# A selective-scan layer on one core: bank readers, copies and stages moved, and TensorE's add of the state's product ahead of the jobs in every step

## The reference

```python
t = windows of x                               # (1024, 64, 128)
tn = layernorm(t) * ln_g + ln_b
xi, z = split(tn @ W_in + b_in)                # 256 channels each
xc = silu(causal_conv4(xi) + conv_b)
dr, Bm, Cm = split(xc @ W_x)                   # 8, 16, 16
delta = softplus(dr @ dt_w + dt_b)
h = exp(delta * A) * h + (delta * xc) * Bm     # 16 states per channel, over 64 tokens
y = sum over states of h * Cm, + xc * D
out = (y * silu(z)) @ W_out + b_out + x
```

## Time and profile before

| | us |
|---|---|
| median of 3 runs | 9951.25 (9944.27 to 9953.19) |
| the profiled execution's own time | 9964.25 |
| its span | 9962.4 |
| busy in the span: PE | 8796.7 (88%) |
| DVE | 8381.0 (84%) |
| POOL | 8037.3 (81%) |
| ACT | 7716.3 (77%) |
| mean granted TensorE clock | 0.976 |

### The profile page before, as it was taken

How to read it: one execution, slowest core, us unless ns; L and a number is a source line. 1 busy time by engine, 2 the same in 40 slices (tenths; PEclk the granted TensorE clock), 3 DMA queues, 4 the chain that set the end, 5 groups by cost and what they waited for, 6 DMA issues and landing times. The chain is left out here.

```text
span 9962.4 us, 180628 instructions
## 1 busy us (share of the span) xinstructions
PE 8796.7 (88%) x54525; PEld 6817.5 (68%) x54525; DVE 8381.0 (84%) x8272; ACT 7716.3 (77%) x13798; POOL 8037.3 (81%) x3609
## 2 busy tenths in 40 slices
PE   7888888888888888888888888888889999999899
PEld 4666666666666666666666666666678888888788
DVE  5888888888888888888888888888978888888766
ACT  5888888888888888888888888888845555555577
POOL 5888888888888888888888888888868888888600
PEclk8999999999999999999999999999999999999999
DMA  3333333333333333333333333333310110101165
GB/s 88 106 105 111 104 103 108 107 106 103 106 109 106 103 107 109 106 103 106 107 107 106 106 105 106 105 103 108 104 41 30 34 34 30 34 30 34 56 189 181
DMA packets 648651, 933.96 MB, mean 94 GB/s; under 512 B 79960, under 2 KB 277600, under 8 KB 643552
## 3 DMA queue, kind: packets, MB, share of 16 engines
q1 hardware_dynamic: 647904, 924.64, 29.5%
HBM read 778.38 MB, written 146.04 MB: 93 GB/s over the span
## 5 line engine op out<-in xcount | busy, mean ns | idle before, releaser
L1022 POOL TENSOR_TENSOR prod<-state,c_all 128x1024 f32<-128x1024 f32 x1280 | 3027.4, 2368 | 820.2 <-DVE state L895 792.1
L603 PEld LDWEIGHTS y_acc<-ident,prod 128*128 128x128 f32 x16384 | 1924.0, 144 | 844.7 <-issue 822.8
L895 DVE TENSOR_TENSOR_SCAN state<-decay_d,drive_d 128x1024 f32<-128x1024 f32 x1024 | 2338.0, 2283 | 187.7 <-ACT decay_d L731 156.8
L1011 POOL TENSOR_TENSOR drive_d<-du,b_all 128x1024 f32<-128x1024 f32 x1024 | 2423.7, 2367 | 0.0
L895 DVE TENSOR_TENSOR_SCAN state<-decay_r,drive_r 128x1024 f32<-128x1024 f32 x1024 | 2330.2, 2276 | 3.5 <-issue 1.4
L603 PE MATMUL y_acc<-ident,prod 128*128 128x128 f32 x16384 | 2195.5, 278 | 4.0 <-DVE prod L906 1.9
L1303 DVE SCALAR_TENSOR_TENSOR sum_d<-bank_d,filt,sum_d 128x512 f32<-128x512 f32 x2470 | 1679.5, 744 | 271.3 <-PE bank_d L1211 248.7
L744 ACT ACTIVATE ub<-ut,bt 128x256 f32<-128x256 f32 x4096 | 1737.1, 497 | 41.9 <-issue 28.7
L1350 POOL TENSOR_TENSOR sum_p<-sum_p,scaled 128x1024 f32<-128x1024 f32 x650 | 1554.6, 2392 | 261.0 <-ACT scaled L1261 229.0
L1261 ACT ACTIVATE scaled<-bank_p,filt 128x512 f32<-128x512 f32 x1560 | 945.5, 689 | 737.4 <-PE bank_p L1211 621.4
L590 PE MATMUL drive_r<-ident,ub 128*128 128x128 f32 x8192 | 1127.3, 282 | 344.9 <-DVE state L895 283.4
(11 more groups left out here) (155 smaller groups left out, 14649.4 us busy)
## 6 DMA issues: line engine op xcount, KB each, us to landing
c_all<-bc_rows SPq DMA_DIRECT2D x1280, 256.0 KB, 3.3
b_all<-bc_rows SPq DMA_DIRECT2D x1024, 256.0 KB, 3.6
ys<-row_spectra SPq DMA_DIRECT2D x130, 256.0 KB, 2.8
column_sums<-tt SPq DMA_DIRECT2D x130, 256.0 KB, 2.1
x_in<-in_x_dram SPq DMA_DIRECT2D x64, 512.0 KB, 4.8
x_res<-in_x_dram SPq DMA_DIRECT2D x64, 512.0 KB, 4.4
x_rows<-x SPq DMA_DIRECT2D x64, 512.0 KB, 4.3
row_spectra<-z SPq DMA_DIRECT2D x64, 512.0 KB, 4.8
```

What stands on the lines that cost most here:

```text
L603: mm = pe.matmul(y_acc[:, g, hf * P:(hf + 1) * P], prod[n % NP][:, hf, g * P:(g + 1) * P], wt["ident"][:], start=(n % NS == 0 and hf == 0 ...
L895: dve.tensor_tensor_scan(state[n % NT][:].rearrange("p h t -> p (h t)"), decay[:].rearrange("p h w t -> p (h w t)"), drive[:].rearrange("p ...
L1011: pool.tensor_tensor(drive_d[place_of(DSTEPS, n, ND)][:], du[:, :, q * HT:(q + 1) * HT], b_all[slot][:].unsqueeze(1).to_broadcast([P, 2, HT]),
L1022: pool.tensor_tensor(prod[n % NP][:], state[n % NT][:], c_all[slot][:].unsqueeze(1).to_broadcast([P, 2, HT]), ALU.mult).then_inc(s["prod_g ...
```

## The change

PE's add of step n - 3 goes ahead of the jobs in all 32 steps (`ADD_FIRST`). Around it the tables are changed: four POOL products move (4, 12, 18, 26 become 2, 14, 18, 30), many jobs and readers move by one or more steps, z01 and z11 and bt1 change banks, bt's copy goes from DVE to ACT, `copy_y` goes one step forward and behind the decays and takes in ACT's step, `take_low` one step back. The work on `z1`, fy and `yo` of a block is cut off its stage "back" and becomes a stage "tail", one block later for z1, in steps 1 and 7 and 28, 29, with one more slot at the end.

```diff
-BY_GPSIMD = tuple(sorted(RSTEPS + (4, 12, 18, 26)))
+BY_GPSIMD = tuple(sorted(RSTEPS + (2, 14, 18, 30)))
...
-    (12, "ut11", "scan", 0), (12, "z01", "front", 1), (13, "z11", "front", 1),
-    (14, "out0", "back", 1), (16, "out1", "back", 1),
...
+    (8, "z01", "front", 0), (9, "conv01", "front", 1),
...
+    (12, "ut11", "scan", 0), (13, "out0", "back", 1),
+    (14, "z11", "front", 0), (15, "out1", "back", 1),
...
+    (28, "fy0", "tail", 1), (29, "fy1", "tail", 1),
...
+ADD_FIRST = tuple(range(NSTEP))
...
-    "copy_y": (19, 3), "take_rows": (17, 0), "take_conv": (3, 7, 9, 11), "take_z": (0, 2, 12, 13),
+    "copy_y": (18, 2), "take_rows": (17, 0), "take_conv": (3, 8, 10, 12), "take_z": (0, 2, 8, 14),
...
-    "low": (17, 0), "take_bt": (28, 8), "take_ut0": (24, 26), "take_ut1": (10, 12),
+    "low": (18, 1), "take_ut0": (26, 28), "take_ut1": (10, 12),
...
-    for m in range(blocks - 2, blocks + 1):
-        slot = Slot(m, False, m < blocks - 1, m < blocks, True, rounds)
+    for m in range(blocks - 2, blocks + 2):
+        slot = Slot(m, False, m < blocks - 1, m < blocks, m <= blocks, True, rounds)
...
+                    if n in ADD_FIRST and S.step(n - ADD_BEHIND, p):
+                        add_state(S.step(n - ADD_BEHIND, p))
                     for name in S.at(n):
                         job(S, p, n, name)
                     for name in S.at(n - 1):
                         if name.startswith("conv"):
                             job(S, p, n, name, 1)
-                    if S.step(n - ADD_BEHIND, p):
+                    if n not in ADD_FIRST and S.step(n - ADD_BEHIND, p):
                         add_state(S.step(n - ADD_BEHIND, p))
...
+            def take_bt(S, q):
+                misc = full(act, S, f"bt{q}")
+                act.activation(bt[q][:].rearrange("p g n -> p (g n)"), misc[:, 0:4 * NS],
+                               ACT.Copy).then_inc(take(S, f"bt{q}"), 1)
...
-                    if n == AT["copy_y"][1] and S.back:
-                        copy_y(m - 1, 1)
-                    if n == AT["copy_y"][0] and S.scan:
-                        copy_y(m, 0)
...
+                    if n == AT["copy_y"][1] and S.back:
+                        copy_y(m - 1, 1)
+                    if n == AT["copy_y"][0] and S.scan:
+                        copy_y(m, 0)
+                    if n == AT["take_bt"][1] and S.scan:
+                        take_bt(S, 1)
+                    if n == AT["take_bt"][0] and S.front:
+                        take_bt(S, 0)
```

More of the change, by code:

```diff
@@ L73 @@
     (4, "turn10", "back", 0), (4, "dt01", "scan", 1), (5, "dt11", "scan", 1),
[11 rows of a table removed]
-]
-SKIP_AT = {3: 0, 5: 1, 13: 2, 15: 3, 19: 0, 25: 1, 29: 2, 31: 3}
[11 rows of a table added]
+]
+SKIP_AT = {4: 0, 6: 1, 13: 2, 15: 3, 19: 0, 23: 1, 27: 2, 31: 3}
+ADD_FIRST = tuple(range(NSTEP))
 AT = {
-    "copy_y": (19, 3), "take_rows": (17, 0), "take_conv": (3, 7, 9, 11), "take_z": (0, 2, 12, 13),
[5 rows of a table removed]
-    "x_in": 14, "rows": (18, 1), "rows_landed": (24, 8), "x1_out": 19, "x_res": 23, "yo_out": 30,
+    "copy_y": (18, 2), "take_rows": (17, 0), "take_conv": (3, 8, 10, 12), "take_z": (0, 2, 8, 14),
[5 rows of a table added]
+    "x_in": 15, "rows": (18, 1), "rows_landed": (24, 8), "x1_out": 18, "x_res": 23, "yo_out": 30,
 }
@@ L130, with __init__ @@
 class Slot:
-    def __init__(self, m, ahead, front, scan, back, rounds):
-        self.m, self.ahead, self.front, self.scan, self.back = m, ahead, front, scan, back
-        on = {"ahead": ahead, "front": front, "scan": scan, "back": back}
+    def __init__(self, m, ahead, front, scan, back, tail, rounds):
+        self.m, self.ahead, self.front, self.scan, self.back, self.tail = m, ahead, front, scan, back, tail
+        on = {"ahead": ahead, "front": front, "scan": scan, "back": back, "tail": tail}
         self.mine = [j for j in JOBS if on[j[2]]]
@@ L161, in slots @@
     for m in range(-2, 2):
-        slot = Slot(m, True, m >= -1, m >= 0, m >= 1, rounds)
+        slot = Slot(m, True, m >= -1, m >= 0, m >= 1, False, rounds)
         body(slot, m % 2)
@@ L532, in body @@
                 m = S.m
-                before, now, after = (place(m + i) if on else None for i, on in
-                                      ((-1, S.back), (0, S.scan), (2, S.ahead)))
+                behind, now, after = (place(m + i) if on else None for i, on in
+                                      ((-2, S.tail), (0, S.scan), (2, S.ahead)))
                 for n in range(NSTEP):
@@ L562, in body @@
                         load_x(x_res, now, s["xres_ready"])
-                    if n == AT["yo_out"] and S.back:
-                        need(sp, s["yo_done"], m)
-                        sp.dma_start(yv[bass.ds(before[1], 1), bass.ds(before[0], 1)]
+                    if n == AT["yo_out"] and S.tail:
+                        need(sp, s["yo_done"], m - 1)
+                        sp.dma_start(yv[bass.ds(behind[1], 1), bass.ds(behind[0], 1)]
                                      .rearrange("o q f r d -> (o q f) r d"), yo[:]).then_inc(s["yo_stored"], 16)
@@ L693, in job @@
                     q = int(name[-1])
-                    need(pe, s["z1_done"], (m - 1) * 2 + q + 1)
+                    need(pe, s["z1_done"], (m - 2) * 2 + q + 1)
                     mm = pe.matmul(misc[:], wt["fy"][:], z1[:, 4 * q:4 * q + 4, :].rearrange("p r c -> p (r c)"),
@@ L822, in behind, with tail @@
                     act.activation(rstd1[:], rstd1[:], ACT.Exp, scale=-0.5).then_inc(s["rstd1_done"], 1)
+            def tail(S, n, m):
                 if n in AT["z1"]:
                     q = AT["z1"].index(n)
-                    need(act, s["yo_stored"], m * 16)
-                    need(act, s["shift1_done"], m)
+                    need(act, s["yo_stored"], (m - 1) * 16)
+                    need(act, s["shift1_done"], m - 1)
                     for r in range(4 * q, 4 * q + 4):
@@ L877, in body @@
                         behind(S, n, m)
+                    if S.tail:
+                        tail(S, n, m)
             act.preload_act_table_set(TABLES)
@@ L925, in take_low @@
                                   c_rows[q][LOW:LOW + NS, :].bitcast(F32), ALU.subtract).then_inc(take(S, f"xp{q}"), 1)
-            def take_bt(S, q):
-                misc = full(dve, S, f"bt{q}")
-                dve.tensor_copy(bt[q][:].rearrange("p g n -> p (g n)"),
-                                misc[:, 0:4 * NS]).then_inc(take(S, f"bt{q}"), 1)
             def take_ut(S, h, q):
@@ L952, in behind @@
                     misc = full(dve, S, f"out{q}")
+                    if q == 0:
+                        need(dve, s["z1_done"], (m - 1) * 2)
                     need(dve, s["x1_stored"], m * 16)
@@ L979, in body @@
                         take_low(S, m + 1, 0)
-                    if n == AT["take_bt"][1] and S.scan:
-                        take_bt(S, 1)
-                    if n == AT["take_bt"][0] and S.front:
-                        take_bt(S, 0)
                     for h in range(2):
```

2 lines of the change are left out of this document (1 added, 1 removed), and 24 rows, old and new, of tables (AT, JOBS).

## The result

The changed kernel takes 10199.15 us (median of 4 runs, 10184.16 to 10220.31), the kernel before 9947.76 on the same chip (9937.46 to 9953.19): a ratio of 1.0256, with a 95% interval of 1.0235 to 1.0276. It is 251 us slower, where 139 were forecast. The profiled execution took 10195.65 us.

A forecast was written before the change was run, and what follows sets the result against it. No engine bounds the whole block: PE's queue sets steps 5 to 17, DVE's scans 18 to 31. Place-by-place gains and losses gave 2.2 us x 63 blocks = 139, so 10090 us; 8 in 10 range 9790 to 10230.

The forecast's parts named there:

- Block start: First scans of a block: broadcast at t = 6.8 instead of 5.91, DVE waits 2.8 instead of 1.92, scan 2 gains 0.3.
- y's copy at add 0: PE waits 1.3 for ACT's copy of y, queued behind z1; a skip and broadcast still owed after turn 5: loss 0.9.
- rival 3: Slower with the clock down: 10216; if yo's store also delays z1 and add 0, about 1 more a block, 10280; chance 0.15.
- Broadcast 8: PE, ready at t = 33.3, waits 1.9 for ACT's take of z01, done at 35.2.
- silu: z11 moved to step 14: take_low 0's wait of 2.48 goes, scan 18 waits 2.35 for decay 18; loss 0.8 by scan 19.
- y's copy at step 18: Copy ends at 73.1, add 16 and dt00 wait behind it, DVE waits 1.3 for gate 0; scan 21 is 1.95 behind.
- the clock term, taken at 0: TensorE clock over the block: falls as often as before, despite PE idling 2.8 before turn 19 and 4.1 before add 16.
- the forecast case: Whole kernel: each place loses its own price, 2.2 us a block, 10090 us; own range 0.8 to 3.4 a block; chance 0.45.
- Rival 1: Whole block: PE has room, add-first costs nothing, take_low 0 and decay_d waits go; 189 us faster, 9760; chance 0.27.
- high price: Clock falling in every block: 4.1 less the 2.1 lost on average now, 2.0 x 63 = 126 us.

The follow-up runs named there:

- the moves alone: The changed kernel with ADD_FIRST empty, so no add goes ahead of the jobs, all moves of jobs, readers and stages kept: 9848.75 us, 0.9904 of the kernel before.

## Why the prediction was right in sign and short in size

t is counted as in the prediction. The block measured here (take_low 1 at 2178.18) is the one whose scan 31 ends at 2169.70: it starts on time, and its take_low 1 starts at t = 8.49 (8.27 to 8.9 in the blocks that start on time).

*Block start.* Forecast: the broadcast at t = 6.8 and a wait of 2.8 on DVE. Measured: the broadcast at 6.6, behind a wait of 1.84, and a wait of 2.88. Right.

*y's copy at add 0.* Forecast: a wait of 1.3. Measured: 1.21 in the 4 blocks that start late, and 1.8 to 2.5 in the 31 others, since z1 waits for the store of yo. The prediction had "find 1.3 us of room" for that store and put the case into rival 3 with a chance of 0.15. ACT comes to z1 at t = 9.0, close to the forecast 9.1, but the store lands at t = 9.7 to 10.1, so there was no room, and ACT was 0.9 us too early on average. In the moves alone z1 waits for the store too (36.0 us in 29 waits), but there the conv half stands ahead of the add. That is **the step that failed first**. The add then carried the lateness to the conv half and turn 5, in 18 of the 35 blocks with the clock on top. Three edits that free these steps (the adds of steps 19 and 3, z1) are worth 147, 143 and 140 us. Rival 3 put the store at about 1 a block and the clock at 2.0; a block with both has 1.1 and 1.7.

*Broadcast 8.* Forecast a wait of 1.9; it was 1.42. The 26 us that came from taking z first say that not more than 0.4 a block of it was on the path, on the kernel with late adds.

*silu.* Forecast at t near 59 with scan 18 at 68.45. Measured in the block of 2169.70, from ACT's timeline:

```profile
2231.12 1.28 ACT L796 ACT_TABLE_LOAD   x1
```

That is t = 61.4, which less the 2.7 by which this block's first part is longer (64.58 less 61.90) is 58.7; scan 18 starts at 2240.44, t = 70.7, less the same 2.7: 68.1. Both right within half a microsecond. The prediction booked a loss of 0.8 there by scan 19 and called the gain that the moves promise at this place gone. With z11 at step 13 the time is 131 to 152 us lower, 2.1 to 2.4 a block: most of the 2.5 that had been there to win.

*y's copy at step 18.* Forecast: gate 0 at t = 77.9, scan 21 at 78.55. Measured in the same block, less the same 2.7: the copy ends at t = 72.7, forecast 73.1, gate 0 starts at 79.1 and scan 21, at 2252.06, at 79.7. So the copy was 0.4 early and the gate 1.2 late, and between them dt00, a skip and turn 21 took some 1.6 longer than at a granted clock of 1.00 (3.85 from start to start, where such pieces take 0.86, 0.44 and 0.87; dt00 lasts 1.56 for 1.02, and the clock is 0.68 from 2245 to 2249). This is the 1.0 by which the smallest parts are longer than forecast (112.2 for 111.2), and it is the second step that failed: **the clock term, taken at 0**. Between 8 us before take_low 0 and 12 us behind it the granted clock falls to 0.50 in all 35 blocks, for 8.4 us on average (from 20 windows of 1 us a block, twice what is missing to 1); before the change it did so in 11 of 36, for 1.4 on average (the earlier trace rows show such a fall, a mean of 0.60 and an add of 1.91). The idle times that the prediction named there, 2.8 and 4.1, were seen (2.78, and 2.64 to 4.0); that the clock would fall behind them no more often than before was not so. In other blocks the gate comes 9.65 behind take_low 0 and has waited 3.88, with the granted clock lower still (busy windows of 14 us, clock before the DMA share; the second is of such a block):

```profile
2238.00:2252.00 14.00, 10.16 (x52) 8.38 (x52) 8.58 (x13) 12.32 (x24) 8.74 (x4) 0.76 0.50 153
...
3381.00:3395.00 14.00, 9.73 (x51) 8.30 (x52) 8.03 (x12) 12.04 (x24) 8.46 (x4) 0.63 0.48 155
```

*The two adds together.* The prediction's terms are 0.9 at add 0 and, at add 16, what its 1.95 holds beyond the 0.8 that it had already lost by scan 19, so about 1.15: 2.05 a block, some 130 us. (78.55 less 76.64 is 1.91, not 1.95.) Both adds back behind their jobs give 2.85 on the smallest parts and 3.75 on the mean, 250 us in all, nearly twice as much. Singly neither step takes more than 0.6 off the smallest parts, so the two prices were not independent.

*The sum.* Forecast 2.2 x 63 = 139, measured 251: 3.15 x 63 = 198 in the undisturbed block, of it 63 from the stretch behind add 16, 33 are the difference to the 231 between the two profiled executions, and 20 more the one to the medians. In the window the mean block exceeds the undisturbed one by 2.6 before and by 2.6 after (the prediction had 2.1 before, from 4000 / 36 for a mean period that is 111.6; and its block of 109.04 did not repeat "to the hundredth": 8 of 35 come within 0.2 of it). So the prediction was right that disturbances would cost the same on average, but by luck: the old ones went, and new ones came, at steps 1 to 5, that three edits could take away. The measured 10199 lies above the forecast case's own range (10000 to 10165), 17 below rival 3's 10216; it lies in the range of 8 in 10 because that took in a part of rival 3.

*The rivals.* Rival 1's half "the moves pay" is true: 99 us, about half of its 189. Its other half, add-first costs nothing, is false by 350. The forecast held the two in one sum and so never said that the first was a gain: each place was costed with both edits in force, and that hid it. Rival 3 is in good part what happened, the store late and the clock down; it had a chance of 0.15. The share of the span at a granted clock of 0.50, estimated from the means of 0.976 and 0.960 as twice what is missing to 1, rose from 4.8% to 8.0%, about 340 us more at the low level. How much of the 251 us this is stays open: at most half of the 340 is lost work of PE (the add of 2240.61 lasts 1.91 at 0.50, the one of 2170.84 1.04 at 1.00), and not all of it was on the path. A kernel that keeps PE busy in those waits would tell; it was not tried. The prediction set the clock aside with "I take 0", though the time with its high price, 10216, came nearest. No run shows that price, 2.0 a block, by itself. What the runs show in its place: PE idles and its clock falls around take_low 0 in every block, but at steps 3 to 5 only in 18 of the 31 blocks with the long wait, 1.7 in the block of 3092.20. PE's weight loads were busy 32.8 of the 45.2 us in the earlier trace rows, 72%; the 350 us here for an order that adds no work to PE speak against counting the other 28% as free room.

## What to carry to other kernels

In this kernel the order in PE's queue alone cost 329 to 350 us, with no work added. Put ahead only what is ready when the queue comes to it; an instruction that waits for another engine's long chain (here y's copy behind z1, decays and ub on ACT) goes behind work that waits for nothing: two such adds of 32 cost 202 to 250 us. Time the parts of a bundled change apart: here a gain of 99 us was covered by a loss of 350, and with three more edits (z11, the order of two takes, z1) the gain became 282. When a step moves ahead of a wait, look at the slack of everything that this wait had covered, stores and their queues included. Read the periods as a distribution: the sum of the smallest parts can be a block that never occurs.

## What was unexpected of the hardware

- The clock fell behind some waits on PE and not behind others of the same length in the same place. Behind waits of 2.0 to 2.5 us for y's copy at step 3 the conv half lasted 3.08 us in the block of 3092.20 (granted clock 0.50 from 3100 to 3103) and 1.82 in that of 2750.30 (1.00 from 2756 to 2762); in the window 18 of the 31 blocks with the long wait have the fall. Some 15 us before the wait of 2.29 of the block of 3092.20 PE had waited 2.34 and went on at 1.00 (from 3083.9 to 3087). So the length of one wait doesn't decide it; what does stays open. The rows: the block of 2750.30, then the earlier wait.

```profile
2756.70 1.09 PE L604 MATMUL y_acc<-ident,prod 128*128 128x128 f32 x8 [2.35 <-ACT y_tok L820]
2757.63 1.82 PE L641 MATMUL job_bank<-x_in,tap_w 128*128 128x496 f32 x4
```

```profile
3083.95 1.09 PE L591 MATMUL drive_r<-ident,ub 128*128 128x128 f32 x8 [2.34 <-DVE state L911]
3084.87 1.04 PE L604 MATMUL y_acc<-ident,prod 128*128 128x128 f32 x8
```

- The prices of reorderings don't add: 147 and 143 us singly, 250 together, since each freed the same steps; z1 behind the copy is worth 140 us on the change and 26 on the kernel that has neither.
- A store that always landed at the same place in the block, t = 9.7 to 10.1, cost time or not by when ACT came to wait for it: a block that started 2 us late did not feel it.
- The mean granted clock goes with the time of the kernel from end to end, 0.952 (10272 us) to 0.983 (9649 us, both the profiled executions), with the same work in all of these kernels. It does not rank them in between: the run of 9925 us has 0.968, the kernel before with 9964 has 0.976.
